# Down products of two expert tiles side by side on TensorE's row halves, with the odd tiles' weights fetched by SyncE

## The reference

```
def _L0_ffn_ref(hidden_states, ...):          # E, F, K = 64 experts, 64 hidden, 8 chosen of 64
    tidx, tw = _gate(x, gate_w, gate_bias)    # 8 experts for each row, and their weights
    for each expert e:
        hmid = silu(x @ We_gate[e]) * (x @ We_up[e])      # 128 -> 64
        y = y + weight[:, e] * (hmid @ We_down[e])        # 64 -> 128
    return y + silu(h @ Ws_gate) * (h @ Ws_up) @ Ws_down
```

## Time and profile before

| | us |
|---|---|
| median of 3 runs | 1664.81 (1664.76 to 1666.91) |
| profiled execution, its own time | 1664.28 |
| its span, first to last instruction | 1662.5 |
| PE busy | 1575.8 (95%) |
| DVE busy | 1199.7 (72%) |
| ACT busy | 777.1 (47%) |
| POOL busy | 670.6 (40%) |
| mean granted TensorE clock | 0.983 |

### The profile page before, as it was taken

One profiled execution on the slowest core, in us unless ns is written; L12 is line 12 of the kernel. 1 busy time (PEld: TensorE's weight loads), 2 busy tenths in 40 slices (PEclk: granted clock), 3 DMA queues, 4 the chain that ended last, 5 costly groups with the idle time before them and its releaser, 6 DMA issues. The chain is left out here.

```text
span 1662.5 us, 27254 instructions
## 1 busy us (share of the span) xinstructions
PE 1575.8 (95%) x8683; PEld 1017.4 (61%) x8683; DVE 1199.7 (72%) x3446; ACT 777.1 (47%) x2105; POOL 670.6 (40%) x931
## 2 busy tenths in 40 slices
PE   5899999999999899999999998997998999999999
PEld 2444444444888677777777776774447896444443
DVE  4687888765455478899898978764776855778675
ACT  2333223222444477777777766774224443223222
POOL 1000088887000323443333205544881002888840
PEclk9999999999899899999999999999999999999999
DMA  9999555552566300010000001103464765656652
GB/s 184 198 254 231 146 130 141 137 142 76 152 189 189 97 17 25 25 28 22 21 22 24 14 1 33 38 31 96 117 153 132 194 188 138 145 139 147 150 132 64
DMA packets 202043, 181.31 MB, mean 109 GB/s; under 512 B 39408, under 2 KB 154288, under 8 KB 201904
## 3 DMA queue, kind: packets, MB, share of 16 engines
q1 hardware_dynamic: 175056, 132.34, 33.3%
q0 software_dynamic: 16384, 33.59, 7.3%
q10 hardware_dynamic: 10464, 13.63, 2.5%
HBM read 121.83 MB, written 57.67 MB: 108 GB/s over the span
## 5 line engine op out<-in xcount | busy, mean ns | idle before, releaser
L840 ACT ACTIVATE f_hid<-banks 128x512 f32<-128x512 f32 (+1 forms) x264 | 157.6, 597 | 502.0 <-PE banks L800 501.7
L481 POOL DMA_INDIRECT x_rows<-r_xk,r_idx x256 | 266.1, 1040 | 139.8 <-issue 53.6
L862 DVE TENSOR_TENSOR f_hid<-banks,f_hid 128x512 f32<-128x512 f32 (+1 forms) x264 | 181.5, 688 | 153.5 <-ACT f_hid L840 153.2
L796 PE MATMUL banks<-r_xT_d,gu 128*128 128x512 f32 x528 | 276.0, 605 | 3.9 <-DMA wd<-in_L_ffn_We_down 2.3
L812 PE MATMUL banks<-f_hid,wd 128*128 128x512 f32 x528 | 272.2, 599 | 5.7 <-DVE f_hid L875 5.6
L800 PE MATMUL banks<-r_xT_d,gu 128*128 128x512 f32 x528 | 273.9, 601 | 0.0
L517 POOL DMA_INDIRECT f_g<-y_rows,r_idx x128 | 129.8, 1014 | 161.8 <-DMA y_rows<-f2q_yq 132.3
L875 DVE TENSOR_TENSOR f_hid<-f_mix_wide,f_hid 128x512 f32<-128x512 f32 x256 | 175.6, 686 | 26.0 <-DMA f_mix_wide<-mix_rows 23.7
L517 POOL DMA_INDIRECT a_g<-y_rows,r_idx x128 | 125.2, 978 | 160.6 <-POOLq L1602 105.6
L812 PEld LDWEIGHTS banks<-f_hid,wd 128*128 128x128 f32 x528 | 99.6, 192 | 140.4 <-issue 123.1
L800 PEld LDWEIGHTS banks<-r_xT_d,gu 128*128 128x128 f32 x528 | 100.9, 191 | 130.1 <-issue 127.0
(11 more groups left out here) (237 smaller groups left out, 2842.4 us busy)
## 6 DMA issues: line engine op xcount, KB each, us to landing
f_mix_wide<-mix_rows SPq DMA_DIRECT2D x124, 512.0 KB, 6.7
x_rows<-zero ACTq DMA_DIRECT2D x12, 1024.0 KB, 6.2
f1q_xq<-x_rows SPq DMA_DIRECT2D x48, 256.0 KB, 3.1
y_rows<-f1q_yq SPq DMA_DIRECT2D x48, 256.0 KB, 2.4
f2q_xq<-x_rows SPq DMA_DIRECT2D x48, 256.0 KB, 3.1
y_rows<-f2q_yq SPq DMA_DIRECT2D x48, 256.0 KB, 2.4
x_rows<-r_xk,r_idx POOLq DMA_INDIRECT x256
wd<-in_L_ffn_We_down SPq DMA_DIRECT2D x7, 512.0 KB, 9.9
```

The source lines that it names most:

```text
L481: nc.gpsimd.indirect_dma_start(x_rows[:, :], bass.IndirectOffsetOnAxis(ap=b.idx[:, f, CT * k + t, j:j + 1], axis=0), b.xk[:, k, t, :], Non ...
L796: nc.tensor.matmul(gate_bank[g % 3][0:rows, :], w["gu"][:, 0, experts, :].rearrange("p e f -> p (e f)"), x, start=True, stop=True)
L840: nc.scalar.activation(d.hid[0:rows, g % HIDS, :], gate_bank[g % 3][0:rows, :], ACT.Silu)\
L862: nc.vector.tensor_tensor(d.hid[0:rows, g % HIDS, :], up_bank[g % 3][0:rows, :], d.hid[0:rows, g % HIDS, :], ALU.mult).then_inc(gated, 1)
```

## The change

Even tiles use partitions 0 to 63 and odd tiles partitions 64 to 127 of hidT, down weights and TensorE's rows, and the two write into different banks: an even tile's result to bank 5, an odd tile's to bank 6. hidT has 128 partitions and half the columns, and one ScalarE copy takes both halves. The even tiles' weights stay where they are in `wd`. For the odd tiles the expert's weights must lie on partitions 64 to 127; SyncE fetches them from DRAM for each quad, two transfers of 64 rows of 512 B, at an address from a register which it loads from `ids_in` (a copy of the tile owners, held below 64), into one of six buffers `wd_high`. They count on the same semaphore as the quad's x, which `turn` waits for. Both banks serve every quad, so `down(j)` waits until quad j - 1 has been read. Core of the diff:

```diff
 YBUFS, STORE_LAG, GBUFS = 3, 6, 3
+HIGH_BUFS = 6
 HALVES = (range(0, TOPK // 2), range(TOPK // 2, TOPK))
...
 SPARSE_STEPS = 23
-PLAN_STEPS = 12
+PLAN_STEPS = 13
 PLACE_STEPS = 4
...
 WEIGH_STEPS = W_STEPS * CT + 5
...
     b.owner, b.ids = sb("owner", [P, CT]), sb("ids", [P, CT], I32)
+    b.ids_in = sb("ids_in", [P, CT], I32)
     return b
...
                 ins = V.tensor_reduce(b.owner[:, :], b.behind[:, :, :], AX_X, ALU.add)
+            elif i == 11:
+                ins = V.tensor_copy(b.ids[:, :], b.owner[:, :])
             else:
-                ins = V.tensor_copy(b.ids[:, :], b.owner[:, :])
+                ins = V.tensor_scalar(b.ids_in[:, :], b.owner[:, :], float(E - 1), None, ALU.min)
             ins.then_inc(plan_step, 1)
...
         def place(k, i):
...
-def quads(ctx, nc, tag, w, x_all, banks, b, q, x_rows, y_rows, r, chunk_of, before_banks=()):
+def quads(ctx, nc, tag, w, x_all, banks, b, q, x_rows, y_rows, r, chunk_of, wd_rows, before_banks=()):
...
     A, B = (banks[0], banks[1]), (banks[2], banks[3])
-    C, ends = banks[4], (banks[5], banks[6])
+    C = banks[4]
+    ends = banks[8].rearrange("p (s j n d) -> p s j n d", s=2, j=2, n=CT // 2)[:, :, 0]
     loaded = [sem(f"loaded{i}") for i in range(3)]
...
     hid_done, hid_turned, y_done = sem("hid_done"), sem("hid_turned"), sem("y_done")
-    hT_copied = [sem("hT_even_copied"), sem("hT_odd_copied")]
+    hT_copied = sem("hT_copied")
     y_read = sem("y_read")
...
                 i = j - SPARSE
-                pe.wait_ge(loaded[i % 3], 16 * (i // 3 + 1))
+                pe.wait_ge(loaded[i % 3], 48 * (i // 3 + 1))
             if j >= 2:
...
             for t in range(CT):
...
             if j >= 1:
-                pe.wait_ge(hT_copied[0], j)
-                pe.wait_ge(hT_copied[1], j)
+                pe.wait_ge(hT_copied, j)
             for u in range(2):
...
             e = expert.pop(j)
-            pe.wait_ge(hT_copied[0], j + 1)
-            pe.wait_ge(hT_copied[1], j + 1)
-            if j >= 2:
-                pe.wait_ge(y_read, j - 1)
+            pe.wait_ge(hT_copied, j + 1)
+            if j >= 1:
+                pe.wait_ge(y_read, j)
+            i = j - SPARSE
             for t in range(CT):
-                wt = w["wd"][0:F, e[t], :] if j < SPARSE else \
-                    w["wd"][0:F, bass.ds(e[t], 1), :].rearrange("p a h -> p (a h)")
-                mm = nc.tensor.matmul(ends[j % 2][:, t * P:(t + 1) * P], q.hidT[:, j % 2, t, :], wt,
+                n, side = divmod(t, 2)
+                rows = slice(side * F, (side + 1) * F)
+                if i < 0:
+                    wt = w["wd"][rows, E, :]
+                elif side:
+                    wt = q.wd_high[rows, i % HIGH_BUFS, n, :]
+                else:
+                    wt = w["wd"][rows, bass.ds(e[t], 1), :].rearrange("p a h -> p (a h)")
+                mm = nc.tensor.matmul(ends[:, side, n, :], q.hidT[rows, j % 2, n, :], wt,
                                       start=True, stop=True)
...
-        def copy_odd(j):
+        def copy_hidT(j):
             act.wait_ge(hid_turned, j + 1)
...
                 act.wait_ge(y_done, j - 1)
-            nc.scalar.copy(q.hidT[:, j % 2, 1::2, :], C[F:P, 0:2 * P].rearrange("p (t n) -> p t n", n=P))\
-                .then_inc(hT_copied[1], 1)
+            nc.scalar.copy(q.hidT[:, j % 2, :, :], C[:, 0:2 * P].rearrange("p (t n) -> p t n", n=P))\
+                .then_inc(hT_copied, 1)
...
             if ok(j):
...
             if ok(j - 2):
-                copy_odd(j - 2)
+                copy_hidT(j - 2)
...
-        def copy_even(j):
-            dve.wait_ge(hid_turned, j + 1)
-            if j >= 2:
-                dve.wait_ge(y_done, j - 1)
-            nc.vector.tensor_copy(q.hidT[:, j % 2, 0::2, :], C[0:F, 0:2 * P].rearrange("p (t n) -> p t n", n=P))\
-                .then_inc(hT_copied[0], 1)
-
         def take_y(j):
...
             if j < SPARSE:
-                x = x_all[:, chunk_tiles(chunk_of[j]), :].rearrange("p t d -> p (t d)")
-                nc.vector.scalar_tensor_tensor(x, ends[j % 2][:, :], 0.5, x, ALU.mult, ALU.add).then_inc(y_read, 1)
+                x = x_all[:, chunk_tiles(chunk_of[j]), :].rearrange("p (n s) d -> p s n d", s=2)
+                for side in range(2):
+                    ins = nc.vector.scalar_tensor_tensor(x[:, side], ends[:, side], 0.5, x[:, side],
+                                                         ALU.mult, ALU.add)
+                ins.then_inc(y_read, 1)
                 return
...
                 dve.wait_ge(y_stored[i % YBUFS], 16 * (i // YBUFS))
-            nc.vector.tensor_copy(q.yq[:, i % YBUFS, :, :].rearrange("p t d -> p (t d)"), ends[j % 2][:, :])\
+            nc.vector.tensor_copy(q.yq[:, i % YBUFS, :, :].rearrange("p (n s) d -> p n s d", s=2),
+                                  ends.rearrange("p s n d -> p n s d"))\
                 .then_inc(y_read, 1)
...
                 gated(j - 1)
-            if ok(j - 2):
-                copy_even(j - 2)
             if ok(j - 3):
...
+        def load_high(i):
+            if i == 0:
+                sp.wait_ge(r.plan_step, PLAN_STEPS - 1)
+            if i >= HIGH_BUFS:
+                sp.wait_ge(y_done, SPARSE + i - HIGH_BUFS + 1)
+            _, expert = nc.values_load_multi_w_load_instructions(
+                b.ids_in[i:i + 1, 1::2], engines=SP_ONLY, min_val=0, max_val=E - 1,
+                skip_runtime_bounds_check_because="the smaller of 63 and a count of experts")
+            for n in range(CT // 2):
+                sp.dma_start(q.wd_high[F:P, i % HIGH_BUFS, n, :],
+                             wd_rows[bass.ds(expert[n], 1), :, :].rearrange("a f h -> (a f) h"))\
+                    .then_inc(loaded[i % 3], 16)
+
         def store(i):
...
             sp.dma_start(rows(y_rows, i), q.yq[:, i % YBUFS, :, :]).then_inc(y_stored[i % YBUFS], 16)
...
                 load(i)
+                load_high(i)
             if i >= STORE_LAG:
...
     q.xq, q.xqT = sb("xq", [P, 3, CT, D]), sb("xqT", [P, 2, CHUNK])
+    q.wd_high = sb("wd_high", [P, HIGH_BUFS, CT // 2, D])
     q.sg, q.hid = sb("sg", [P, 2, CT * F]), sb("hidq", [P, 2, CT * F])
-    q.hidT, q.yq = sb("hidT", [F, 2, CT, P]), sb("yq", [P, YBUFS, CT, D])
+    q.hidT, q.yq = sb("hidT", [P, 2, CT // 2, P]), sb("yq", [P, YBUFS, CT, D])
     return q
...
         dn = dense(ctx, nc, "f1d_", w, x_all, gate_bank, up_bank, acc, misc, d, mix_rows, r, dense_of, ready=ready)
-        qd = quads(ctx, nc, "f1q_", w, x_all, psum, b, q, x_rows, y_rows, r, chunk_of)
+        qd = quads(ctx, nc, "f1q_", w, x_all, psum, b, q, x_rows, y_rows, r, chunk_of, dr["wd"])
         block = ctx.enter_context(nc.Block())
...
         @block.tensor
...
-def ffn_second(nc, w, x_all, psum, b, mix_rows, x_rows, y_rows, r, out, dispatched, gathered, added):
+def ffn_second(nc, w, x_all, psum, b, mix_rows, x_rows, y_rows, wd_rows, r, out, dispatched, gathered, added):
...
     dense_of = [q for q in SECOND if q.dense >= 0]
...
         stored, misc_rows = sem("stored"), Misc()
-        qd = quads(ctx, nc, "f2q_", w, x_all, psum, b, q, x_rows, y_rows, r, chunk_of)
+        qd = quads(ctx, nc, "f2q_", w, x_all, psum, b, q, x_rows, y_rows, r, chunk_of, wd_rows)
         dn = dense(ctx, nc, "f2d_", w, x_all, gate_bank, up_bank, acc, misc, d, mix_rows, r, dense_of,
...
         block = ctx.enter_context(nc.Block())
...
         banks = ctx.enter_context(nc.psum_tensor("banks", [P, 8 * 512], F32))
-        psum = [banks[:, i * 512:(i + 1) * 512] for i in range(8)]
+        psum = [banks[:, i * 512:(i + 1) * 512] for i in range(8)] + [banks[:, 5 * 512:7 * 512]]
         b = persistent_buffers(ctx, nc)
...
             attention(nc, w, x_all, banks, psum, rows, b, mix_rows, y_rows, first, second, gathered, added)
-        ffn_second(nc, w, x_all, psum, b, mix_rows, x_rows, y_rows, second, out_v, tiles // (SEQ // P) * (H // 4) - A_DISPATCH,
+        ffn_second(nc, w, x_all, psum, b, mix_rows, x_rows, y_rows, We_down, second, out_v, tiles // (SEQ // P) * (H // 4) - A_DISPATCH,
                    gathered, added)
```

More of the change, by code:

```diff
@@ L14 @@
 PE_ONLY = [mybir.EngineType.PE]
+SP_ONLY = [mybir.EngineType.SP]
 P = 128
```

## The result

| | before | after |
|---|---|---|
| median, us | 1665.86 (4 runs, 1664.76 to 1668.29) | 1726.70 (4 runs, 1721.39 to 1733.14) |
| ratio to before | | 1.0369 [1.033, 1.0408] |
| span of the profiled execution, us | 1662.5 | 1731.4 |

The forecast was 1656 us, a small gain. The time is 46 us above the upper end of the range, 1681.

The account below looks back on a forecast made before the run. TensorE bounds the sparse stages at 2.78 us a step; after the change SyncE's queue would, at 2.75. Gain 7.5 + 8.0 = 15.5 us, less 6.4 for long pushes, leaves 9.1: 1656 us; 8-in-10 range 1623 to 1681.

Parts of the forecast that it names:

- The row halves: TensorE's down block: records go in four pairs, block from 1.08 to 0.64 us, step from 2.78 to 2.34.
- the pushes are cheap: Rival: SyncE's pushes cost little, TensorE stays the bound at 2.34 us a step; 1623 us, chance 0.10.
- y_read, VectorE's cover, the copy of hidT: Single set of result banks and merged copies: `down` waits for the previous quad's copy, 0.9 us of cover, cost nothing.
- The last quad's way through the pipeline: End of each stage: 7.6 us less four down blocks at 0.44 gives 5.9, with a little waiting 6.0.
- SyncE's queue becomes the bound: SyncE's work per step sums to 2.74, say 2.75 us, above TensorE's new 2.34; bounds 2.0 and 3.3.
- store with what follows: SyncE's queue, each step: pushing the store of y and what comes behind it, priced at 0.40 us.
- register load up to the address work: SyncE's load from `ids_in`: 0.34 us as on TensorE's queue, some 0.16 until the first address computation, together 0.50.
- two address computations: SyncE's queue, each step: addresses for the two weight transfers at 0.05 us each, 0.10 in all.
- two pushes of weights: SyncE's queue, each step: two 64-row transfers at 0.55 and 0.60 us plus 0.04, 1.19 in all.
- From step to time: Each stage: six steps at 2.35, forty-two at 2.75, less 0.4, plus 8.1 at the end: 137.3 us.
- Long pushes: SyncE's occasional slow loads, eight of 96, 6.4 us over in all, formerly in idle time, now counted fully.
- SyncE's step is longer than TensorE's old one: Rival: register work or its load costs more; above 2.845 us a step it loses, at 3.0 1680 us; chance 0.29.

Follow-up runs that it names:

- experiment 1: Changed kernel without the weight transfers: odd tiles use the shared expert's down weights and `turn` waits for x alone; 1622.91 us, ratio 0.9737.
- experiment 2: Changed kernel with the experts of the two transfers fixed at build time, so no register work on SyncE; 1645.30 us, ratio 0.9873.
- experiment 5: Changed kernel with SyncE's register load moved ahead of the load of x, stores still on SyncE; 1679.29 us, ratio 1.0088.
- experiment 7: Changed kernel with experts fixed at build time and the stores of y pushed by ScalarE, six buffers; 1640.68 us, ratio 0.9851.
- experiment 8: Changed kernel with experts fixed at build time, stores of y pushed by ScalarE, and ten buffers instead of six; 1626.63 us, ratio 0.9769.

## Why the prediction was wrong

*The row halves: right.* TensorE's step went to 2.34 us (experiment 1) and so the block from 1.08 to 0.64, as the attention rows had said. Experiment 1's 1622.9 stands beside the 1623 of the rival "the pushes are cheap", but the agreement is in part luck: that sum took off 1.5 us a stage for a wait that experiment 1 doesn't have, and missed some 1.9 us a stage at the end (next paragraph).

*y_read, VectorE's cover, the copy of hidT: right in the middle of a stage, wrong at its end.* No wait for them is among TensorE's in 440 to 550 us, and experiment 1 has both edits. But the cover of 0.9 us was counted from the blocks that lie between two down blocks, and at the end of a stage these run out: TensorE waits 0.98 us for y and 0.48 for hidT. The last quad's way through the pipeline was forecast at 5.9, with waiting 6.0 us; in experiment 1 it took 7.8 in both stages. This is small beside the rest, and it was priced at nothing.

*SyncE's queue becomes the bound: right.* The size of the sum was wrong, 3.59 for 2.74 us:

| term | priced | measured, step from 484.78 | |
|---|---|---|---|
| store with what follows | 0.40 | 0.63 | +0.23 |
| load of x with what follows | 0.55 | 0.56 | 0 |
| register load up to the address work | 0.50 | 1.07 | +0.57 |
| two address computations | 0.10 | 0.28 | +0.18 |
| two pushes of weights | 1.19 | 1.05 | -0.14 |

**The step that failed is the price of the register load**, 0.50 us, taken from TensorE's queue, where little else is pushed; here it was 1.07. Its upper bound, that queue's longest 0.68, did not hold either, so the bound of 3.3 us for the step was too low. On SyncE's queue two values cost 0.46 us at best, and 0.87 in the median. The range's upper end, a step of 3.0, fell with it. The second failed term is the store. Its 0.36 us was read where the queue had waited for `y_read` before each push; pushed right behind another transfer it takes 0.58. I had seen this surcharge for the load (0.51 against 0.36) and didn't carry it to the store when I took its wait away. The third is the address work: each transfer has a computation of 0.04 us, a move of 0.03 and the time between them, 0.14 us in all where 0.05 was priced. The two 64-partition pushes took 0.48 and 0.47 us for a priced 0.55 and 0.60. That pushes and second address computation together come to the priced 1.19 is luck.

The Trainium skill, "DMA: Bandwidth & Descriptors", section "Latency and other measured facts", gives the register load about 600 ns; my estimate from it was 1681. It erred in the right direction, but no run here shows such a floor: 0.26 us for one value and 0.46 for two are below it, and 0.87 is above.

*From step to time: right for the steps, short for the ends.* The steps with stores average (164.5 - 6 x 2.46) / 41 = 3.65 us in the first stage and (163.6 - 6 x 2.50) / 41 = 3.62 in the second, for 2.75: 73 us over. The six steps without stores took 2.46 and 2.50 in the mean for 2.35: 1.6 us over. From the last push of x to the last down product it was 16.2 and 12.7 us, forecast 10.5 each: 8 us over. Less the 6.4 us of long pushes that the forecast had as a term of its own this is 76 us, and 1655.2 + 76 = 1731 for the profiled execution, which took 1733.1. The median of the four runs is 6 us lower.

*Long pushes: priced at 6.4 us, too low.* Before, 8 of SyncE's 192 pushes in these stages took over 0.85 us, 6.4 us over the usual ones in all. In the changed kernel 17 of 384 did, 15.5 us over, and in experiment 2 18 of 384, 15.6 over. The forecast carried the count of before to twice as many pushes. The DMA share, 0.58 in the changed kernel and 0.83 in experiment 2, made no difference to their number in these two executions.

*The rivals.* The one that came true, "SyncE's step is longer than TensorE's old one", had 0.29. (Of the two forms in which the prediction gives the forecast's own range, 1646 to 1666 follows from its steps of 2.65 to 2.85, and 1644 to 1667 does not.) For the cheap pushes I had set beside it the Trainium skill, "DMA: Bandwidth & Descriptors", section "Issuing engines are not separate DMA queues", by which the issue time is usually small. Here a push of 32 KB took 0.47 to 0.60 us beside a landing of 2.1, and with four of them a step the issue time is the bound even without register work (experiment 2, 2.41 us a step beside TensorE's 2.34). For these sizes the trace disagrees.

**What stays open:** why the register load is long. The runs show when: 0.2 to 1.4 us after the end of a store's push, from whichever queue, and not right behind it (experiment 5). What it waits for there, no view shows, and a run that moves only the store's time was not made.

## What to carry to other kernels

An in-order queue whose waits vanish has to be priced instruction by instruction in its new neighbourhood: a push behind a push, a register load shortly after a store, and the queue's rare long instructions too, which idle time had hidden and of which twice the pushes brought twice the number here. A wait whose cover is counted from the middle of a pipeline has to be counted again for its end. Before data is fetched anew for each tile, look for a copy on the chip and an idle engine to move it: here that was worth 105 us against the same idea done with transfers. If a register load must stand in such a queue, its place is worth an experiment: one moved line gave 47 us.

## What the hardware showed that I had not expected

- A register load of two values took 0.46 to 1.25 us on SyncE's queue. Of those over 0.7 us, 210 of 211 had started 0.2 to 1.4 us after the end of a store's push. One value less takes 0.2 us off.
- The push of the same 256 KB transfer took 0.36 us into a queue that had waited, 0.37 with a register load in front of it and 0.50 to 0.59 right behind another push.
- The landing of a 32 KB transfer rose from 2.1 us (changed kernel, DMA share 0.58) to 2.8 (experiment 2, 0.83), 3.0 (experiment 7, 0.84) and 3.3 (experiment 8, first stage, 0.88).
- A wait of TensorE can cost its clock. After one of 2.59 us the same blocks ran at the 1.2 GHz level, gate and up in 1.90 us instead of 1.06, and were back at the 2.4 GHz level some 4 us later. The same place of the second stage follows, and then the window of the slow stretch:

```profile
586.79 0.66 PE L580 MATMUL banks<-ident,f1q_xq 128*128 128x128 f32 x4 [2.59 <-DMA f1q_wd_high<-in_L_ffn_We_down]
587.73 1.90 PE L605 MATMUL banks<-gu,f1q_xqT 128*128 x8 [0.29 <-issue]
...
591.15 1.25 PE L605 MATMUL banks<-gu,f1q_xqT 128*128 x8
```

```profile
1454.71 1.15 PE L605 MATMUL banks<-gu,f2q_xqT 128*128 x8 [0.31 <-issue]
...
1456.66 1.16 PE L605 MATMUL banks<-gu,f2q_xqT 128*128 x8
```

```profile
587.70:590.90 3.20, 3.17 (x18) 2.84 (x18) 0.42 (x1) 1.12 (x3) 0.00 (x0) 0.54 0.23 70
```

The window's granted clock is 0.54. This is the last quad of the stage, and nothing behind it hides the slow blocks: from gate and up to the next it is 3.42 us, and 1.95 in the second stage, so the clock cost this execution about 1.5 us here. Over both stages the granted clock is 0.95, for 0.98 and 1.00 before. In their middle TensorE waits in most steps anyway (27 times in 110 us), so I take the clock there for no part of the loss; that was not tested.
